# First pairs of a fused attention and experts kernel: an own key scale, a shorter first block, and another order of stores and loads

## The reference

```python
x = x + tanh(g_xattn[0]) * attention(layernorm(x), ctx, ctx, mask, Wq, bq, Wk, bk, Wv, bv, Wo, bo)   # 16 heads of 8
x = x + tanh(g_ffn[0]) * experts(layernorm(x), rW, rb, W1, b1, W2, b2, sW1, sb1, sW2, sb2)
# attention: softmax(q k^T / sqrt(8), masked keys at -1e10) v, then @ Wo + bo
# experts: mean of 2 shared ones + the best 2 of 8 with softmax weights; each is gelu(x @ W1 + b1) @ W2 + b2, 512 wide
```

## Time and profile before

| what | us |
|---|---|
| median of 3 runs (lowest, highest) | 455.94 (453.99, 456.85) |
| the profiled execution's own time | 454.94 |
| its span | 453.1 |
| busy: PE, DVE, ACT, POOL | 386.3, 384.9, 340.8, 309.7 |

### The profile page before, as it was taken

The page is one execution under the profiler, slowest core; times in us unless marked ns, Lnnn a source line. Parts: engine busy times, 40 slices in busy tenths (PEclk is TensorE's granted clock), DMA queues, the critical chain, the costliest instruction groups (busy, mean ns, idle before and its releaser), DMA issues.

```text
span 453.1 us, 14622 instructions
## 1 busy us (share of the span) xinstructions
PE 386.3 (85%) x5155; PEld 316.6 (70%) x5155; DVE 384.9 (85%) x947; ACT 340.8 (75%) x677; POOL 309.7 (68%) x431
## 2 busy tenths in 40 slices
PE   0558889997999899988789999998999999999910
PEld 0335677786788788766557776777899999999900
DVE  7696668978876987899778999887799999999986
ACT  0635677787888788878789986775888888888844
POOL 6252222799899899978777767774177777777740
PEclk9999999999999999999899999999999999999975
DMA  7968884354333334474221111112223333355229
GB/s 192 314 196 214 206 186 110 90 138 98 92 92 98 87 95 107 101 229 175 92 66 49 55 37 53 49 48 69 70 83 96 97 90 93 94 156 158 69 78 294
DMA packets 71686, 53.43 MB, mean 118 GB/s; under 512 B 7209, under 2 KB 63476, under 8 KB 71616
## 3 DMA queue, kind: packets, MB, share of 16 engines
q1 hardware_dynamic: 64896, 43.15, 35.9%
q0 software_dynamic: 4544, 8.44, 5.6%
q10 hardware_dynamic: 2176, 0.91, 0.8%
HBM read 29.51 MB, written 24.33 MB: 119 GB/s over the span
## 4 chain that ended last, share of the span: by engine, by line
POOL 23%; PE 21%; DVE 20%; issue 13%; DMA 10%; SPq 6%; ACT 4%; POOLq 0%; DVEq 0%; ACTq 0%
POOL yd L650 9%; DVE HH L1533 5%; PE pAtt L1144 4%; DMA scr<-QKS 4%; PE pAtt L1090 2%; PE pS L1132 2%; PE pE L1132 2%; DVE t_MX L1257 2%; POOL t_STG L558 2%; POOL t_W2l L562 2%; POOL QKS L548 2%; PE pAtt L928 1%; DMA t_STG<-in_W 1%; POOL xs L628 1%; POOL t_XF L572 1%
## 5 line engine op out<-in xcount | busy, mean ns | idle before, releaser
L650 POOL DMA_INDIRECT yd<-Y,XR x78 | 86.8, 1113 | 37.6 <-issue 23.2
L1257 DVE TENSOR_REDUCE t_MX<-pS 128x4 f32<-128x512 f32 x128 | 86.8, 682 | 22.6 <-PE pS L889 20.0
L748 ACT ACTIVATE PT<-pE,t_mbias,t_scl 128x512 f32<-128x512 f32 x128 | 96.9, 789 | 2.7 <-PE pE L889 2.7
L628 POOL DMA_INDIRECT xs<-t_STG,t_pos x64 | 66.2, 1034 | 23.1 <-issue 14.3
L1563 DVE SCALAR_TENSOR_TENSOR HR<-GG,t_sc,HR 128x512 f16<-128x512 f32 x78 | 58.6, 751 | 2.8
L1144 PE MATMUL pAtt<-t_W2h,HR 128*128 x624 | 59.2, 219 | 0.7 <-DVE HR L1563 0.7
L889 PE MATMUL pS<-t_K,t_Q 128*128 128x128 f16 x512 | 52.0, 228 | 8.5 <-DVE t_MX L1257 5.1
L1144 PE MATMUL pAtt<-t_W2l,HR 128*128 x312 | 54.4, 219 | 0.0
L828 ACT ACTIVATE GG<-pS,t_b1T,t_inv 128x256 f32<-128x256 f32 x78 | 39.8, 561 | 16.9 <-PE pS L1132 16.9
L889 PE MATMUL pE<-t_Q,t_K 128*128 128x128 f16 x512 | 49.9, 220 | 1.6 <-DMA t_Q<-MPl 0.6
L1144 PEld LDWEIGHTS pAtt<-t_W2h,HR 128*128 128x128 f16 x624 | 49.6, 98 | 1.1 <-issue 0.9
(11 more groups left out here) (280 smaller groups left out, 1042.7 us busy)
## 6 DMA issues: line engine op xcount, KB each, us to landing
xs<-t_padrow SPq DMA_DIRECT2D x10, 516.0 KB, 5.1
XR<-xs SPq DMA_DIRECT2D x39, 129.0 KB, 2.3
scr<-QKS SPq DMA_DIRECT2D x16, 256.0 KB, 2.4
t_Q<-scr SPq DMA_DIRECT2D x16, 256.0 KB
t_K<-scr SPq DMA_DIRECT2D x32, 128.0 KB
t_STG<-in_W SPq DMA_DIRECT2D x7, 512.0 KB, 6.6
YY<-yd SPq DMA_DIRECT2D x14, 256.0 KB, 4.2
t_X<-in_x SPq DMA_DIRECT2D x4, 512.0 KB, 7.7
```

Source lines behind the costliest of these rows:

```text
L628: g.indirect_dma_start(k.xs, bass.IndirectOffsetOnAxis(ap=pos[:, n:n + 1], axis=0), k.PAY[:, n, :], None).then_inc(h.di[q], 16)
L650: g.indirect_dma_start(k.yd, bass.IndirectOffsetOnAxis(ap=XR[u][:, q, D:ROW], axis=0), Y[u][:, q, :], None, bounds_check=2 * T - 1, oob_is ...
L748: act.activation(PT[:, m % NPT], pE[g % 2][:], ACT.Exp, bias=k.mbias[:, bt:bt + 1], scale=k.scl[:, bt:bt + 1]).then_inc(s.exp, 1)
L1257: v.tensor_reduce(out=MX[:, n // G % 2, n % G // 4, m % 2, m // 2::2], in_=pS[n % 2][:], axis=AX_X, op=ALU.max).then_inc(s.max, 1)
```

## The change

Pairs 0 to 7 get a key scale of their own. It comes from context chunks 0 and 1 alone, as the root of the largest sum of squares in a partition: ACT squares the chunks at the end of the prologue, and DVE's four maxima go. Pairs 8 to 15 get a second key scale in turn 6 (`other_keys_scale`), from maxima that DVE takes in turns 2 and 3.

The loads of Wv, Wo, the biases and the router move on ACT from the prologue to behind the copy of pair 0's transposes, and the two gates' loads to the front. The clearing of the buffers of pairs 2 and 3 moves on ACT from ahead of queries and keys 0 to behind queries and keys 1. On SP the stores and loads of pair 0 stand ahead of the last tokens, the weights and the padding of the other buffers. The squares of the weights move from turn 1 to turn 2 (0 and 1 in step 3; 2, 3 and 4 in step 7), and the statistics of token chunks 2 and 3 from turn 0 to turns 2 and 3. PE's and POOL's instructions keep their order.

The diff, cut to its core:

```diff
+OWN_CHUNKS = 2
+OWN_PAIRS = OWN_CHUNKS * 4
...
-TOPS = 3
+TOPS = 4
...
+                for dst, src in gates:
+                    a.dma_start(dst, src).then_inc(s.gw, 16)
                 for dst, src in first:
                     a.dma_start(dst, src).then_inc(s.first, 16)
-                for dst, src in gates:
-                    a.dma_start(dst, src).then_inc(s.gw, 16)
-                for dst, src in rest:
-                    a.dma_start(dst, src).then_inc(k.s_rest, 16)
-                a.wait_ge(s.km, 1)
-                a.dma_start(k.kmd.rearrange("(b s) -> b s", s=S), k.kmrow[:]).then_inc(k.s_one, 16)
                 a.wait_ge(s.gw, 16 * len(gates))
-                a.activation(k.gt[:], graw[:], ACT.Tanh).then_inc(s.gl, 1)
-                a.wait_ge(s.gl, 1)
+                a.activation(k.gt[:], k.graw[:], ACT.Tanh)
+                for n in range(OWN_CHUNKS):
+                    a.wait_ge(k.s_c[n], 16)
+                    a.activation(k.b2[:], k.CC[n].rearrange("p a b -> p (a b)"), ACT.Square, accum_out=k.mx[:, 5 + n:6 + n]).then_inc(k.s_cs, 1)
+                    a.wait_ge(k.s_cs, n + 1)
...
-            for n in range(2, NT // CHUNK):
-                load_tokens(n)
-            for n in range(PIECES - 1):
-                load_weights(n)
-            for u in range(NB):
-                sp.dma_start(k.scr[u][0, :, 3, :], k.constq[:]).then_inc(k.s_pad, 16)
-            sp.wait_ge(k.s_one, 16)
-            key_mask(0)
-            for u in range(NB):
+            def key_padding(u):
+
                 if u == NB - 1:
                     sp.wait_ge(s.zk, 1)
                 for par in range(2):
-                    sp.dma_start(k.K[u][SHIFT + 2 * par:SHIFT + 2 * par + 2, par::2, :], k.constk[:]).then_inc(k.s_padk, 16)
+                    sp.dma_start(k.K[u][SHIFT + 2 * par:SHIFT + 2 * par + 2, par::2, :], k.constk[:]).then_inc(k.s_padk[min(u, 1)], 16)
+
+            for u in range(NB):
+                sp.dma_start(k.scr[u][0, :, 3, :], k.constq[:]).then_inc(k.s_pad, 16)
+            key_padding(0)
+            sp.wait_ge(k.s_one, 16)
+            key_mask(0)
...
+                for later in {0: (1,), 1: range(2, NB)}.get(t, ()):
+                    key_padding(later)
                 if a:
                     sp.wait_ge(s.w[u], N_W * again + N_W)
                     sp.dma_start(k.Q[u][0:SHIFT, :, :], scr[0].rearrange("(h2 pd) s t -> (pd s) h2 t", pd=2 * HD)).then_inc(s.rd[u], 16)
                     for par in range(2):
                         src = scr[1].rearrange("(h2 par d) s t -> par (d s) h2 t", par=2, d=HD)[par]
                         sp.dma_start(k.K[u][SLOT_ROWS * par:SLOT_ROWS * (par + 1), par::2, :], src).then_inc(s.rd[u], 16)
-                for n in {1: range(4, 6), 2: range(6, 8), 3: range(8, 10)}.get(t, ()):
+                if t == 0:
+                    for n in range(2, NT // CHUNK):
+                        load_tokens(n)
+                for n in {0: range(0, 2), 1: range(2, 5), 2: (5,), 3: range(6, 8), 4: range(8, 10)}.get(t, ()):
                     load_weights(n)
...
+                if i == OWN_PAIRS:
+                    act.wait_ge(s.qs, 2)
                 for op in range(2):
-                    ins = act.activation(QK32[:, op, :], pQK(op), ACT.Identity, bias=k.bqk[:, op:op + 1], scale=k.sc[:, op:op + 1])
+                    bias, scale = (2, 6) if op and i >= OWN_PAIRS else (op, op)
+                    ins = act.activation(QK32[:, op, :], pQK(op), ACT.Identity, bias=k.bqk[:, bias:bias + 1], scale=k.sc[:, scale:scale + 1])
                 ins.then_inc(s.qk32, 1)
...
+            act.wait_ge(k.s_km, 1)
+            act.dma_start(k.kmd.rearrange("(b s) -> b s", s=S), k.kmrow[:]).then_inc(k.s_one, 16)
             transposed(0)
-            for u in range(2, NB):
+            for dst, src in k.rest:
+                act.dma_start(dst, src).then_inc(k.s_rest, 16)
+            queries_keys(0)
+
+            def clear_pairs():
+
+                for u in range(2, NB):
+                    clear_one(u)
+                act.wait_ge(s.z, NB - 2)
+                for u in range(2, NB):
+                    ins = act.activation(view(k.V[u], HD, [64, 16], [48, 2], [1, HD]), view(k.ones, 0, [0, 16], [HD, 2], [1, HD]), ACT.Copy)
+                ins.then_inc(s.z, 1)
+
+            def clear_one(u):
+
                 eights = view(k.ones, 0, [0, 8], [1, P])
                 act.activation(k.V[u][:].rearrange("p a b c -> p (a b c)").rearrange("p (n d) -> p n d", d=P), eights, ACT.Copy, scale=0.0)
                 act.activation(k.Q[u][:].rearrange("p a b -> p (a b)").bitcast(F32).rearrange("p (n d) -> p n d", d=P), eights,
-                               ACT.Copy, scale=0.0).then_inc(s.zz, 1)
-            act.wait_ge(s.zz, NB - 2)
-            for u in range(2, NB):
-                ins = act.activation(view(k.V[u], HD, [64, 16], [48, 2], [1, HD]), view(k.ones, 0, [0, 16], [HD, 2], [1, HD]), ACT.Copy)
-            ins.then_inc(s.z, 1)
-            queries_keys(0)
+                               ACT.Copy, scale=0.0).then_inc(s.z, 1)
...
-                    if g == 3 and t == 1:
-                        for n in range(PIECES - 1):
+                    if g == 3 and t == 0:
+                        clear_pairs()
+                    if g == 3 and t == 2:
+                        for n in range(2):
+                            weight_squares(n)
+                    if g == 7 and t == 2:
+                        for n in range(2, PIECES):
                             weight_squares(n)
                     if g == 2 and t == 2:
+                        for sem in k.s_padk:
+                            act.wait_ge(sem, 32 if sem is k.s_padk[0] else 32 * (NB - 1))
                         shifts_out(t)
-                        weight_squares(PIECES - 1)
...
+            pe.wait_ge(s.mb, 2)
             pe.matmul(pA[1][:, 0, 0:5], k.ones[0:5, :], k.mxd[:], start=True, stop=True)
-            pe.matmul(pA[1][:, 1, 0:B], k.ones[:], k.maskT[:], start=True, stop=True).then_inc(s.ma, 1)
+            pe.matmul(pA[1][:, 1, 0:B], k.ones[:], k.maskT[:], start=True, stop=True).then_inc(s.mr, 1)
             pe.wait_ge(k.s_rest, k.rest_in)
...
                 if n == 0:
-                    pe.wait_ge(k.s_padk, 32 * NB)
+                    pe.wait_ge(k.s_padk[0], 32)
+                if n == G:
+                    pe.wait_ge(k.s_padk[1], 32 * (NB - 1))
...
-            for n in range(NT // CHUNK):
-                v.wait_ge(k.s_c[n], 16)
-                ins = absmax(v, k.mx[:, 5 + n:6 + n], k.CC[n].rearrange("p a b -> p (a b)"))
-            link(ins)
-            v.tensor_reduce(out=k.mx[:, 0:1], in_=k.mx[:, 5:9], axis=AX_X, op=ALU.max).then_inc(s.mb, 1)
+            v.wait_ge(k.s_cs, OWN_CHUNKS)
+            v.tensor_reduce(out=k.mx[:, 0:1], in_=k.mx[:, 5:5 + OWN_CHUNKS], axis=AX_X, op=ALU.max).then_inc(s.mb, 1)
...
+            link(v.tensor_scalar(k.mxa[:, 0:1].bitcast(I32), k.mxa[:, 0:1].bitcast(I32), 1, None, ALU.arith_shift_right))
+            link(v.tensor_scalar(k.mxa[:, 0:1].bitcast(I32), k.mxa[:, 0:1].bitcast(I32), 1.0, float(ROOT_ABOVE), ALU.mult, ALU.add))
...
-            def other_deviations():
-
-                first_deviations(v, link, k, CHUNK, NT, tmpv, tmpn)
+            def other_deviations(a, b):
+
+                first_deviations(v, link, k, CHUNK * a, CHUNK * b, tmpv, tmpn)
                 settle(v, s.rs)
+
+            def other_keys_maximum(n):
+
+                v.wait_ge(k.s_c[n], 16)
+                return absmax(v, k.mx[:, 5 + n:6 + n], k.CC[n].rearrange("p a b -> p (a b)"))
...
+            def other_keys_scale():
+
+                link(v.tensor_reduce(out=k.mxa[:, 0:1], in_=view(k.rows, TOPS - 1, [TOPS, P]), axis=AX_X, op=ALU.max))
+                link(v.tensor_tensor(k.tmp2[:, 0:1], k.mxa[:, 0:1], k.mxa[:, 2:3], ALU.mult))
+                link(v.scalar_tensor_tensor(out=k.bound[:, 6:7], in0=k.tmp2[:, 0:1], scalar=float(D), in1=k.mxa[:, 4:5], op0=ALU.mult, op1=ALU.add))
+                scales(v, link, k, 6, 7, 13)
+                link(v.tensor_tensor(k.tmp2[:, 1:2], k.inv[:, 0:1], k.inv[:, 6:7], ALU.mult))
+                link(v.tensor_scalar(k.tmp2[:, 0:1], k.tmp2[:, 1:2], float(HD ** -0.5), None, ALU.mult))
+                v.tensor_scalar(k.scl[:, 2 * OWN_PAIRS:B], k.anyb[:, 2 * OWN_PAIRS:B], k.tmp2[:, 0:1], None, ALU.mult)
+                v.tensor_tensor(k.bqk[:, 2:3], k.bqkr[:, 1:2], k.sc[:, 6:7], ALU.mult).then_inc(s.qs, 1)
...
-                    if t == 0 and g < NT // CHUNK - 1:
-                        chunk_statistics(g + 1)
-                        last = chunk_moments(g + 1)
-                        if g == NT // CHUNK - 2:
-                            link(last)
-                            other_deviations()
+                    if (t, g) in ((0, 0), (2, 4), (3, 3)):
+                        n = ((0, 0), (2, 4), (3, 3)).index((t, g)) + 1
+                        chunk_statistics(n)
+                        link(chunk_moments(n))
```

(8 more changed lines are left out.)

39 lines of the change are left out of this document (21 added, 18 removed).

## The result

The changed kernel takes 472.77 us (median of 4 runs, 472.23 to 473.35), the kernel before, run beside it, 455.21 (453.99 to 456.85): a ratio of 1.038 (95% interval 1.035 to 1.042), slower. The profiled execution of the changed kernel took 472.9, with a span of 471.0 where before had 453.1: 17.9 more. The forecast was 468, range 459 to 474; the direction was right, the size 4.8 short. Busy time hardly moved on three engines (DVE 384.6 against 384.9, ACT 343.4 against 340.8, POOL 309.4 against 309.7), and PE's same 5155 matmuls took 392.4 against 386.3. So most of the 17.9 is waiting, and it was looked for where each engine stands idle.

A forecast was written before the change was run, and what follows sets the result against it. SP's pair-0 rows and the ACT-PE ladder were taken to hold the first score at nearly the same time. Terms 3.4 + 0.8 + 5.0 + 3.3 − 0.85 + 0.8 + 1.0 = +13.5 on 454.94 gave 468; range 459 to 474.

The forecast's parts named there:

- clearing on the ladder: Before the first score: clearing on ACT, 4.63 us, loses its cover except 1.31; the remaining 3.3 delays the ACT-PE sequence.
- turn 2: DVE in turn 2: chunk 2's statistics and one key maximum come in and can delay PE's projection 3; +0.8 (0 to 2.3).
- squares ahead of the first exponential: ACT, end of turn 2: squares 2, 3 and 4 and a wait for weight piece 5 delay it; +5.0 (3.4 to 6.1).
- DVE's piece in turn 3: Chunk 3's statistics and 16 tiles' deviations, 4.9 us between maxima 15 and 16, delay score 18; +3.3 (0 to 4.9).
- waits for keys, turns 4 and 5: PE's wait of 0.85 for pair 3's keys at 63.38 goes, as PE comes later than they: −0.85.
- turn 6, second key scale: Eleven DVE operations, 2.2 us, in turn 6 where DVE is busy 10.5 of 11.5: 0 to 2.2, taken as 0.8.
- clock: PE idle before exponential 0 and in turn 3 drops to half clock, up to 1.6 each; +1.0 (0 to 3.2).
- Queries and keys 0 and the seven loads: Prologue: queries and keys 0 come 0.7 earlier; seven later loads hold pair 0's values; net +0.1 (−0.7 to +4.2).
- Rival 4: Pair 0's scale and rows are not earlier, because the seven loads land at the late end: 472; chance 0.06.
- Rival 3: Array stays slow: gaps in turns 2 and 3 keep PE at half clock, 472 to 475; chance 0.10.
- Rival 1: SP's queue is the bound, so pair 0's earlier rows make the kernel faster: 450; chance 0.05.
- Rival 2: Only the clearing stays; squares and DVE's piece lie beside existing idle time in turns 2 and 3: 458 to 463; chance 0.14.

The follow-up runs named there:

- e1: Changed kernel with the clearing of pairs 2 and 3 back ahead of queries and keys 0: 473.5 us, ratio 1.039.
- e11: Kernel before with the square of weight piece 4 moved to turn 3 and weight pieces 6 to 9 loaded one turn later: 456.5 us, ratio 0.999.
- e2: Changed kernel with squares 2, 3 and 4 moved from ahead of the first exponential into turn 3: 469.6 us, ratio 1.031.
- e3: Changed kernel with token chunks 2 and 3 loaded right behind the first key mask and their statistics in DVE's turn 1: 465.1 us, ratio 1.021.
- e10: Changed kernel with token chunks 2 and 3 loaded right behind the first key mask, statistics left in turns 2 and 3: 469.9 us, ratio 1.026.
- e6: Changed kernel without the second key scale, so pairs 8 to 15 use that of pairs 0 to 7: 469.7 us, ratio 1.029.
- e9: Kernel of e1 with the padding of pairs 1 to 3 issued by SP right behind the first key mask: 473.0 us, ratio 1.034.
- e7: Changed kernel with the 512 KB load of the experts' output bias moved from turn 6 to turn 12: 471.8 us, ratio 1.032.
- e12: Changed kernel with clearing, tokens, padding and chunk 2 and 3 statistics earlier, squares 2 to 4 in turn 3, seven loads on SP: 460.3 us, ratio 1.007.

## Why the prediction was right, and where it was not

The time, 472.8, lies within 459 to 474, but above the 464 to 471 that had a chance of 0.65. The direction, the places and most of the mechanisms came out as predicted; that the time still fell inside is owed to the width of the range, as 3.6 us arose in turns 7 and 8, of which the sum had nothing. The terms of the sum against the trace, each as the growth of the delay over its stretch:

| term | predicted | measured |
|---|---|---|
| clearing on the ladder, to queries and keys 2 | 3.4 | 2.64 |
| turn 2, to queries and keys 3 | 0.8 | 2.76 |
| squares ahead of the first exponential | 5.0 | 4.81 (10.21 − 5.40) |
| DVE's piece in turn 3, to queries and keys 4 | 3.3 | 5.01 (15.22 − 10.21) |
| waits for keys, turns 4 and 5 | −0.85 | −1.61 |
| turn 6, second key scale | 0.8 | 2.13 |
| turns 7 and 8 | 0 | 3.64 |
| behind turn 8, to the end of the span | 0 | −1.48 |
| clock | 1.0 | not a term of its own |
| sum | 13.5 | 17.9 |

*Queries and keys 0 and the seven loads.* This was right: 0.46 earlier against 0.7. PE now waits 0.79 for the last of the seven loads, where it went on at once before, but a wait for queries and keys 0 stands behind that anyway (1.48, 1.96 before). PE's rows, before and after:

```profile
20.86 0.33 PE L881 MATMUL pOut<-t_identf,t_b1r 40*128 40x40 f32 x1
```

```profile
20.89 0.32 PE L908 MATMUL pOut<-t_identf,t_b1r 40*128 40x40 f32 x1 [0.79 <-DMA t_rb<-in_rb]
```

Rival 4 did not occur.

*The clearing.* The mechanism and the place were right, PE's wait there grew by 3.1 (3 predicted), and 0.75 too much was charged. That SP's earlier rows of pair 0 go unused was right too. What the prediction missed is that SP's order has a second effect: the 2 MB moved from ahead of pair 0 to ahead of pair 1. It looked for who waits for pair 0's rows and did not follow the same queue on to pair 1. So undoing the clearing alone (e1) gave nothing.

*Turn 2 on DVE.* This was mis-sized: of the 2.76, 1.04 is that late pair 1 (from the first score to score 8 it takes 8.42 instead of 7.38), and the other 1.7 is put down to the statistics and the key maximum by score 11, which waits 1.81 for DVE there. The upper bound, 2.3, was nearer than the 0.8 taken; the argument that ACT's wait for piece 5 leaves room there was wrong, as e11 also shows: taking that square away from the kernel before moved queries and keys 3 not at all (0.64 behind at 2, 1.14 at 3).

*The squares.* This was right to 0.2, the wait for piece 5 too (square 4 at 59.00, exponential at 60.06). e2 gives back about two thirds of it in time.

*DVE's piece in turn 3.* The piece itself was right (maxima 5.86 apart, 5.6 predicted). It cost 1.7 more than the 3.3. In that stretch the array ran at half clock for much of the time: products took 0.61 from 60.87 on and 0.39 only from 72.9, and the clock is 0.71. From the first exponential to queries and keys 4 it takes 8.1 in the kernel before, 8.8 in e3, which has a stretch of half clock there but not the piece, and 13.1 in e10 and in the changed kernel, which have the piece. So the piece is worth 4.3 together with the half clock behind it, and the half clock ahead of it about 0.7; no run took the piece away and kept the half clock behind it, so how the 4.3 divides is not shown. The Trainium skill, "TensorE: Matmul & The Clock Gate", section "HAM oscillation — how this bites in real kernels", has waits between bursts put the array back to half clock. The clock of 0.50 from 60 to 64, where PE's wait of 4.46 ends, and the 0.50 from 56 to 60 in e3, where one of 5.11 ends, agree. Rival 3, which rested on it, put the time at 472 to 475, where it came out; but the trace puts 5.8 of the 17.9 in turns 6 to 8, with the clock at 1.00 in turns 6 and 7, so the time fits that rival for another reason. Its premise that the first scores run at half rate in any case did not hold either: in e1 they take 0.40 from 39.43 on and in e3 from 41.57 on.

*The second key scale.* This was mis-sized: it was taken at 0.8 of a bound of 2.2, though the profile had DVE busy 10.5 of 11.5 there. e6 makes it 2.4 in turns 6 and 7, over the bound.

*Turns 4 and 5, and the weights in turn 4.* The wait for keys goes as predicted and one like it in turn 5 too. The weights in turn 4, put at nothing, stand ahead of the tops' rows on SP: DVE waits 0.77 for them in turn 5, and 1.59 in e11. The row that waits behind a moved transfer had to be looked up there as well.

*Turn 8.* The prediction had nothing of it, and it is 2.7 of the 4.4 by which the sum is short. Its cause stays open. The second key scale puts the 512 KB load 1.45 behind queries and keys 7, and rows that a waiting product needs stand behind it; but with the load at the same place turn 8 took 12.7 in e9, as much as with the load gone (e7) and 0.15 less than in the kernel before. Some of the 2.7 may belong to that one execution.

Rival 1 fell with the first score. Rival 2 (the squares and DVE's piece are hidden) fell with e2, e3 and e10.

## What to carry to other kernels

When a queue is reordered so that one item goes first, follow everything that it overtakes to the next item that stands behind it: here 2 MB moved from ahead of pair 0, whose rows nobody was waiting for, to ahead of pair 1, whose rows somebody was. A price undone alone can come out at zero because another wait stands at the same height, so price a part both ways: taken out of the change and put alone into the kernel before. Small operations on an engine that is busy nine tenths of a stage cost nearly their full time there (2.4 of 2.7 here). And before a stall in one trace is put down to an instruction, the same place is worth a look in every other trace that has that instruction: turn 8 took 12.7 to 15.6 with the same load at the same place.

## What was not expected of the hardware

- Behind a 512 KB broadcast load in turn 6, SP could load the next scratch rows 11.5 to 13.3 us after the load's issue in thirteen traces, whether it had issued the stores for them 1.5 or 3.1 after it; behind the same load in turn 12 (e7) it was 8.7. From the issue of 8 KB of shifts to the product that used them 6.8 us passed in the changed kernel (116.30 to 123.11), 5.0 in e9 and 4.0 in e7, without the load ahead.
- Two loads of 512 KB moved on SP beside loads that ACT issues delayed those by 3.1 and 3.5 us (PE's wait for them 3.92 in e3 and 4.29 in e10 against 0.79).
- A store of 384 KB took 6.3 us from its last issue to the load that waits for it behind 2 MB of other transfers (e9, 35.17 to 41.52); behind 1 MB of weights it took 6.2 (e12, 32.62 to 38.83); in the kernel before pair 1's took 3.9 (33.23 to 37.17).
